# A decoder layer on one core: the q and k stacks built through DRAM from doubled, contiguous stores

## The reference

```
q = (query @ Wq.T + bq).reshape(B, T, H, D)      # H = 16, D = 16
k = (key   @ Wk.T + bk).reshape(B, S, H, D)
scores = einsum('bhtd,bhsd->bhts', q, k) * scale + attn_mask + 2 * bias_of_head
probs  = softmax(scores);  out = einsum('bhts,bhsd->bhtd', probs, v) @ Wo.T + bo
x = x + attn(ln(x));  x = x + xattn(ln(x), ctx);  x = x + ffn(ln(x))
```

## Time and profile before

| | us |
|---|---|
| three runs: median (lowest, highest) | 2261.62 (2259.73, 2263.55) |
| profiled execution, its own time | 2262.71 |
| span of its trace | 2260.9 |
| TensorE matmuls busy | 2077.8 |
| ScalarE busy | 2024.0 |
| VectorE busy | 1860.7 |
| GpSimd busy | 1780.8 |

### The profile page before, as it was taken

One profiled execution on the slowest core, in us unless ns is written; L12 is line 12 of the kernel. 1 busy time (PEld: TensorE's weight loads), 2 busy tenths in 40 slices (PEclk: granted clock), 3 DMA queues, 4 the chain that ended last, 5 costly groups with the idle time before them and its releaser, 6 DMA issues.

```text
span 2260.9 us, 73067 instructions
## 1 busy us (share of the span) xinstructions
PE 2077.8 (92%) x24128; PEld 1806.0 (80%) x24128; DVE 1860.7 (82%) x6768; ACT 2024.0 (90%) x5937; POOL 1780.8 (79%) x1899
## 2 busy tenths in 40 slices
PE   4679999999999999999999999999999999999877
PEld 2568888888888888888888888888888888888755
DVE  4578888888888888888888888888888888888763
ACT  5689999999999999999999999999999999999862
POOL 2358888888888887888888888888888888777863
PEclk9789999999999999999999999999999999999987
DMA  4388778778877779767776887677788777789860
GB/s 142 114 191 175 159 156 172 162 170 188 172 157 154 175 157 175 183 162 169 163 173 156 182 185 164 165 169 169 161 176 187 159 168 165 169 152 183 172 129 15
DMA packets 711784, 367.16 MB, mean 162 GB/s; under 512 B 561392, under 2 KB 659952, under 8 KB 711408
## 3 DMA queue, kind: packets, MB, share of 16 engines
q1 hardware_dynamic: 711408, 362.50, 72.4%
HBM read 202.98 MB, written 25.17 MB: 101 GB/s over the span
## 4 chain that ended last, share of the span: by engine, by line
PE 61%; issue 11%; POOL 10%; ACT 8%; DMA 5%; DVE 5%; SPq 1%; ACTq 0%; DVEq 0%; POOLq 0%
PE ps_c_hidden L978 15%; PE ps_a_misc L978 14%; PE ps_c_out L978 14%; PE ps_b_misc L1115 5%; DMA b_probsT_hi_lo<-b_probs_hi_lo 5%; PE ps_b_scores L1101 3%; POOL bias L522 3%; PE ps_a_misc L1057 3%; ACT c_relu L684 2%; PE ps_a_scores L1038 2%; ACT ps_b_probs L658 2%; POOL ctxT_hi L488 2%; ACT a_qT_hi L603 1%; POOL a_qT_lo L480 1%; POOL ctxT_lo L491 1%
## 5 line engine op out<-in xcount | busy, mean ns | idle before, releaser
L522 POOL TENSOR_TENSOR bias<-bias,b_mask 128x512 f32<-128x512 f32 x512 | 645.0, 1274 | 6.2 <-DMA bias<-in_bias 5.8
L838 DVE CUSTOM_DVE_ANT_0 b_neg_scores<-ps_b_scores,bias 128x256 f32<-128x256 f32 x1024 | 391.2, 419 | 68.3 <-POOL bias L522 34.2
L845 DVE TENSOR_TENSOR b_probs_hi_lo<-ps_b_probs,b_probs_hi_lo 128x512 f16<-128x512 f32 x512 | 351.7, 687 | 107.3 <-ACT b_probs_hi_lo L666 104.9
L543 POOL TENSOR_TENSOR c_hidden_lo<-c_hidden,c_hidden_hi 128x512 f16<-128x512 f32 x288 | 335.1, 1163 | 48.4 <-issue 32.8
L978 PE MATMUL ps_c_hidden<-c_xT_hi,w_hi 128*128 128x256 f16 x1152 | 317.2, 275 | 19.9 <-ACT c_relu L684 19.9
L536 POOL TENSOR_TENSOR c_hidden<-c_relu 128x512 f32<-128x512 f32 x288 | 299.7, 1041 | 32.4 <-ACT c_relu L684 13.1
L978 PE MATMUL ps_c_out<-w_hi,c_hidden_hi 128*128 128x256 f16 x1152 | 315.6, 274 | 9.9 <-DVE acc L949 9.9
L978 PE MATMUL ps_c_hidden<-c_xT_hi,w_lo 128*128 128x256 f16 x1152 | 316.8, 275 | 0.0
L978 PE MATMUL ps_c_hidden<-c_xT_lo,w_hi 128*128 128x256 f16 x1152 | 316.7, 275 | 0.0
L978 PE MATMUL ps_c_out<-w_hi,c_hidden_lo 128*128 128x256 f16 x1152 | 315.9, 274 | 0.0
L978 PE MATMUL ps_c_out<-w_lo,c_hidden_hi 128*128 128x256 f16 x1152 | 315.8, 274 | 0.0
(11 more groups left out here) (194 smaller groups left out, 7491.0 us busy)
## 6 DMA issues: line engine op xcount, KB each, us to landing
bias<-in_bias SPq DMA_DIRECT2D x256, 512.0 KB, 4.2
q_stack<-qk_scratch SPq DMA_DIRECT2D x256, 64.0 KB, 2.5
x_ln<-in_x SPq DMA_DIRECT2D x32, 256.0 KB, 4.4
ctxT<-in_ctx SPq DMA_DIRECT2D x32, 256.0 KB, 4.4
x<-in_x SPq DMA_DIRECT2D x32, 256.0 KB, 5.5
qk_scratch<-b_qT_hi_lo SPq DMA_DIRECT2D x32, 256.0 KB, 4.5
qk_scratch<-b_kT_hi_lo SPq DMA_DIRECT2D x32, 256.0 KB, 3.7
k_stack_even<-qk_scratch SPq DMA_DIRECT2D x128, 64.0 KB, 2.5
```

What stands on the lines that cost most here:

```text
L522: gp.tensor_tensor(part, part, b_mask[:, :], ALU.add).then_inc(b_c_ok, 1)
L543: gp.tensor_tensor(c_hl[:, u, :], c_h[:, :], c_hh[:, u, :], ALU.subtract).then_inc(c_h_ok, 1)
L838: last = dve.tensor_tensor_reduce(out=b_t[:, u, c, :], in0=ps_bs[:, c * T:(c + 1) * T], in1=bias[:, slot, at:at + T], scale=-2.0, scalar=3 ...
L845: dve.tensor_tensor(b_p2[:, j % DEPTH, :, 1, :], ps_bp[:, :].rearrange("p (c t) -> p c t", c=CT), b_p2[:, j % DEPTH, :, 0, :], ALU.subtrac ...
```

## The change

Two things change together. On the host, the columns of Wq and Wk (and their biases) are permuted, so that the projection puts the 16 features of all even heads into partitions 0 to 63 and those of all odd heads into 64 to 127, with the pairs next to each other. And the scratch tensor in DRAM gets the layout of the stacks themselves: half (even or odd head), row of the stack, feature, pair, tokens. Each store writes one half of the partitions to two of the four rows of the stack, so every part is written twice, in pieces of 1 KB: four stores for q and four for k, where there was one each. Each stack is then read by DMAs whose source is contiguous: one for `q_stack` (128 partitions x 4 KB) and one for each k stack (64 partitions x 4 KB), where there were sixteen. The semaphore counts follow.

```diff
             def b_store_k(b, _):
                 sp.wait_ge(b_kl_ok, after(b, 1, 1))
                 carry_waits(sp)
-                sp.wait_ge(b_kst_ok, after(b, STACK, 0))
-                sp.dma_start(stk_d[1].rearrange("r m p t -> p r m t"), b_k2[:, :, :, :]).then_inc(b_k_dram, 16)
+                sp.wait_ge(b_kst_ok, after(b, 32, 0))
+                for h in range(2):
+                    for u in range(2):
+                        sp.dma_start(stk_d[1, h].rearrange("(r u) d g m t -> u (d g) r (m t)", u=2)[u],
+                                     b_k2[64 * h:64 * h + 64, :, :, :].rearrange("p r m t -> p r (m t)")).then_inc(b_k_dram, 16)

             def b_store_q(b, _):
                 sp.wait_ge(b_ql_ok, after(b, 1, 1))
                 carry_waits(sp)
-                sp.wait_ge(b_qst_ok, after(b, STACK, 0))
-                sp.dma_start(stk_d[0].rearrange("r m p t -> p r m t"), b_q2[:, :, :, :]).then_inc(b_q_dram, 16)
+                sp.wait_ge(b_qst_ok, after(b, 16, 0))
+                for h in range(2):
+                    for u in range(2):
+                        sp.dma_start(stk_d[0, h].rearrange("(u r) d g m t -> u (d g) r (m t)", u=2)[u],
+                                     b_q2[64 * h:64 * h + 64, :, :, :].rearrange("p r m t -> p r (m t)")).then_inc(b_q_dram, 16)

             def b_stack_k(b, _):
-                sp.wait_ge(b_k_dram, after(b, 16, 16))
+                sp.wait_ge(b_k_dram, after(b, 64, 64))
                 carry_waits(sp)
                 sp.wait_ge(b_s_ps, after(b, BH, 0))
-                for head, k in enumerate((k_even, k_odd)):
-                    for r in range(4):
-                        at = 64 * head + BD * r
-                        sp.dma_start(k[at:at + BD, :, :],
-                                     stacked(1, r % 2, head)).then_inc(b_kst_ok, 16)
+                for h, k in enumerate((k_even, k_odd)):
+                    sp.dma_start(k[64 * h:64 * h + 64, :, :],
+                                 stk_d[1, h].rearrange("r d g m t -> (r d) (g m) t")).then_inc(b_kst_ok, 16)

             def b_stack_q(b, _):
-                sp.wait_ge(b_q_dram, after(b, 16, 16))
+                sp.wait_ge(b_q_dram, after(b, 64, 64))
                 carry_waits(sp)
                 sp.wait_ge(b_s_ps, after(b, BH, 0))
-                for head in range(2):
-                    for r in range(4):
-                        at = 64 * head + BD * r
-                        sp.dma_start(q_stack[at:at + BD, :, :],
-                                     stacked(0, r // 2, head)).then_inc(b_qst_ok, 16)
+                sp.dma_start(q_stack[:, :, :],
+                             stk_d[0].rearrange("h r d g m t -> (h r d) (g m) t")).then_inc(b_qst_ok, 16)
...
+    rows_of = np.array([[(2 * (2 * g + m) + h) * BD + d for h in range(2) for d in range(BD) for g in range(PAIRS // CD)]
+                        for m in range(CD)]).reshape(D)
     wpair = [chunks(a["L0_attn_Wq"].T), chunks(a["L0_attn_Wk"].T), chunks(a["L0_attn_Wv"].T),
-             chunks(a["L0_xattn_Wq"].T), chunks(a["L0_xattn_Wk"].T), chunks(a["L0_xattn_Wv"].T),
+             chunks(a["L0_xattn_Wq"].T[:, rows_of]), chunks(a["L0_xattn_Wk"].T[:, rows_of]), chunks(a["L0_xattn_Wv"].T),
...
-        "bq": a["L0_xattn_bq"].reshape(CD, P).T,
-        "bk": a["L0_xattn_bk"].reshape(CD, P).T,
+        "bq": a["L0_xattn_bq"].reshape(D)[rows_of].reshape(CD, P).T,
+        "bk": a["L0_xattn_bk"].reshape(D)[rows_of].reshape(CD, P).T,
...
-    args.append(nc.dram_tensor("qk_scratch", (2, 2, CD, P, T), F16, kind="Internal").ap())
+    args.append(nc.dram_tensor("qk_scratch", (2, 2, 4, BD, P // (2 * BD), CD, T), F16, kind="Internal").ap())
```

More of the change, by code:

```diff
@@ L298, in build @@
         FIX = 7
-        STACK = 16 * 8
         def carry_waits(eng):
@@ L388, in b_store_q @@
                 carry_waits(sp)
-                sp.wait_ge(b_qst_ok, after(b, STACK, 0))
-                sp.dma_start(stk_d[0].rearrange("r m p t -> p r m t"), b_q2[:, :, :, :]).then_inc(b_q_dram, 16)
-            def stacked(kind, part, head):
-                return stk_d[kind, part].rearrange("m (p h d) t -> h d (m p) t", h=2, d=BD)[head]
+                sp.wait_ge(b_qst_ok, after(b, 16, 0))
[3 more added lines that the diff above has]
+                                     b_q2[64 * h:64 * h + 64, :, :, :].rearrange("p r m t -> p r (m t)")).then_inc(b_q_dram, 16)
             def b_stack_k(b, _):
-                sp.wait_ge(b_k_dram, after(b, 16, 16))
+                sp.wait_ge(b_k_dram, after(b, 64, 64))
                 carry_waits(sp)
                 sp.wait_ge(b_s_ps, after(b, BH, 0))
-                for head, k in enumerate((k_even, k_odd)):
-                    for r in range(4):
-                        at = 64 * head + BD * r
-                        sp.dma_start(k[at:at + BD, :, :],
-                                     stacked(1, r % 2, head)).then_inc(b_kst_ok, 16)
+                for h, k in enumerate((k_even, k_odd)):
+                    sp.dma_start(k[64 * h:64 * h + 64, :, :],
+                                 stk_d[1, h].rearrange("r d g m t -> (r d) (g m) t")).then_inc(b_kst_ok, 16)
             def b_stack_q(b, _):
-                sp.wait_ge(b_q_dram, after(b, 16, 16))
+                sp.wait_ge(b_q_dram, after(b, 64, 64))
                 carry_waits(sp)
                 sp.wait_ge(b_s_ps, after(b, BH, 0))
-                for head in range(2):
-                    for r in range(4):
-                        at = 64 * head + BD * r
-                        sp.dma_start(q_stack[at:at + BD, :, :],
-                                     stacked(0, r // 2, head)).then_inc(b_qst_ok, 16)
+                sp.dma_start(q_stack[:, :, :],
+                             stk_d[0].rearrange("h r d g m t -> (h r d) (g m) t")).then_inc(b_qst_ok, 16)
             def b_pT_load(b, j):
@@ L496, in b_split_k @@
                 gp.wait_ge(b_kf_ok, after(b, 2, 2))
-                gp.wait_ge(b_k_dram, after(b, 16, 0))
+                gp.wait_ge(b_k_dram, after(b, 64, 0))
                 gp.tensor_tensor(b_k2[:, 1, :, :], b_kf[:, :, :], b_k2[:, 0, :, :], ALU.subtract).then_inc(b_kl_ok, 1)
@@ L503, in b_split_q @@
                 gp.wait_ge(b_qf_ok, after(b, 2, 2))
-                gp.wait_ge(b_q_dram, after(b, 16, 0))
+                gp.wait_ge(b_q_dram, after(b, 64, 0))
                 gp.tensor_tensor(b_q2[:, 1, :, :], b_qf[:, :, :], b_q2[:, 0, :, :], ALU.subtract).then_inc(b_ql_ok, 1)
@@ L632, in b_kv @@
                 act.wait_ge(b_k_ps, after(b, 1, 1))
-                act.wait_ge(b_k_dram, after(b, 16, 0))
+                act.wait_ge(b_k_dram, after(b, 64, 0))
                 for m in range(CD):
@@ L639, in b_q @@
                 act.wait_ge(b_q_ps, after(b, 1, 1))
-                act.wait_ge(b_q_dram, after(b, 16, 0))
+                act.wait_ge(b_q_dram, after(b, 64, 0))
                 for m in range(CD):
@@ L1095, in b_s @@
                 if j == 0:
-                    pe.wait_ge(b_qst_ok, after(b, STACK, STACK))
-                    pe.wait_ge(b_kst_ok, after(b, STACK, STACK))
+                    pe.wait_ge(b_qst_ok, after(b, 16, 16))
+                    pe.wait_ge(b_kst_ok, after(b, 32, 32))
                 pe.wait_ge(b_t_ok, after(b, BH, j))
```

## The result

The changed kernel takes 2288.28 us (median of four runs: 2282.74, 2282.86, 2293.69, 2293.97) against 2261.77 of the kernel before, measured beside it: ratio 1.0118, interval 1.0082 to 1.0153. It is slower by 1.2%. The prediction was 2284 us, within 2258 to 2306. The profiled execution is the one of 2293.97 us, with a span of 2292.2; the four runs lie in two pairs 11 us apart.

The account below looks back on a forecast made before the run. TensorE's wait for head 15's transposition, queued behind the q store, was taken to bound each batch; 14.5 and 7.7 us of added waits made 22.2, so 2262.7 became 2284.9, as a median 2284 us, range 2258 to 2306.

Parts of the forecast that it names:

- What is added at this wait is added to the batch, one to one: TensorE's wait for head 15's transposition, behind the q store: a 2.0 us wait makes a 65.59 us period into 67.67.
- 0.85 us later per landing: Head 15's transposition behind the q stores: 256 KB more in the DMA engines delay its landing by 0.85 us, bounds 0 and 1.44.
- the sum: Added waits for the transposition: 14.5 us in 17 batches already waiting, 7.7 in 14 others, together 22.2 us.
- From one issue to the next the queue takes 0.48 us: SyncE's queue at the q stores: four issues for one put the transposition's issue 1.44 us later, 1.92 after the first store.
- the issue counts in full: Rival: with the backlog drained, the transposition lands 1.44 us later, 40 us in all, 2302 us; chance 0.12.
- mostly hidden: The transposition's later issue is mostly covered by the DMA backlog ahead of it, so the data decides its landing.
- Half stores at half rate: Rival: 64-partition stores move at half rate, halfway 1.9 us later per landing, 55 us in all, 2316 us; chance 0.12.
- Nothing changes: Rival: time goes by pieces and the issue is hidden; landing within 0.1 us, 2263 us; chance 0.16.
- Faster: Rival: larger, later k store and reads stop disturbing the transposition; half of 22.7 us of waits goes, 2250 us; chance 0.10.
- 2 us or more: Last k read of the stack should land at least this long before TensorE's first score product of the batch.
- A faster stack gains nothing there: Stack reads before the first score product: already in time by under a microsecond, so landing 2 us earlier gains nothing.

Follow-up runs that it names:

- e1: Changed kernel with head 15's transposition issued ahead of the four q stores; 2243.99 us, ratio 0.9916.
- e6: Kernel before, with its q store issued twice at full width, the second copy to scratch that nothing reads; 2302.12 us, ratio 1.0181.
- e7: Changed kernel with q and k stored by two 128-partition DMAs each, same 512 KB, scratch laid out by row, then partition; 2397.88 us, ratio 1.0604.
- e9: e7 with each 64-partition stack read cut into four reads of 16 partitions; 2298.17 us, ratio 1.0152.
- e5: Kernel before, with its q store cut into four half-width DMAs, same 256 KB, nothing doubled; 2268.49 us, ratio 1.0029.
- e10: Changed kernel without the doubling: two half-width stores each for q and k, 256 KB in 1-KB pieces, twelve reads; 2256.86 us, ratio 0.9976.
- e2: Kernel before, with head 15's transposition issued ahead of the one q store; 2260.88 us, ratio 0.9988.

## Why the prediction came out right, step by step

**The place and the sign.** "What is added at this wait is added to the batch, one to one" held to within 0.4 us in 24 of the changed kernel's 30 periods; in five of the others a fall of the clock came on top. TensorE now waits for the transposition in all 31 batches behind a q store, as forecast, and for 41.3 us against a forecast of about 45. That the order of this one transfer is the whole of it is shown by e1: with it first, the k store, the reads, the permuted columns and the counts cost nothing.

**The size of the term.** 0.85 us later per landing was forecast, 0.70 is the mean measured (6.30 to 7.00). By bytes alone it is 0.96 (e6). Whether the pieces of 1 KB give some of that back is not shown: e7 and e9 store the 512 KB of e6 in such pieces and full width and land at 7.04 and 7.16 against 7.26, but within each of these kernels the landings scatter by more than half a microsecond. The landings did not all move by the same amount, as the sum had it: they spread from 5.19 to 8.21 before and from 6.28 to 7.72 after, the early ones moving most. The steady part of the account is 18.7 us of waits where the sum had 22.2.

**What was missed.** The falls of TensorE's clock, 7.9 us of the profiled execution, are in no step of the prediction, nor are the 2 us spread over the other periods and the 2.6 before and after them. In the profiled execution the waits came out 3.5 us below the sum and these 12.6 on top, 31.3 where 22.2 were forecast. The median of the runs is 26.5 above the kernel before, since two of the four are 11 us shorter. That 2284 comes as near to 2288.28 as it does is in part luck: the faster pair alone would have made it too high by 1, the slower one too low by 10. The kernel before has waits of up to 2.2 us without a fall between its second and last store, and no row of it told that longer stalls would bring any.

**The issues.** "From one issue to the next the queue takes 0.48 us" was taken from a full-width store and is wrong for a half-width one: 0.63 and the gap. The transposition is issued 3.16 us after the first store, 1.2 later than forecast. By the forecast's own reckoning, 3.16 + 3.5 = 6.7, the issue alone would bring the landing close to the 7.0 that was measured, so the argument that the backlog hides it had hardly any margin left. The rival that the issue counts in full is refuted by e5 (0.28 us on average for 2.2), but "mostly hidden" was too strong: the same run shows that four issues alone cost 5.1 us of waits. It did no further harm here because the doubled bytes alone bring the landing to the same place (e7, e9).

**The other rivals.** *Half stores at half rate* is refuted: full-width stores of the same bytes land the transposition at 7.04 (e7) and 7.16 (e9), half-width ones at 7.00. The Trainium skill (SBUF — State Buffer, "Door 1: The DMA port swizzle") would have them limited to half of the ports; for these stores, at the 247 GB/s of the whole mix, the trace does not show it. That a narrower limit exists when nothing else moves was not tried. *Nothing changes* went by the count of pieces, 512 before and after; that the landing moved by 0.70 all the same refutes it, in e7 (0.74) as well. *Faster* fell: the fewer reads behind the transposition did not bring its landing forward. e10, with 256 KB and fewer, larger pieces, lands only 0.17 us earlier than the kernel before, which its scatter does not resolve.

**The stack.** In the batch shown the last k read lands at 1106.2 + 4.3 = 1110.5, and the first score product loads at 1111.73: 1.2 us of slack. That is the least of the 30 batches; on average the slack is 3.0 us where the kernel before has 1.2 (0.1 at least). So "2 us or more" held on average and not everywhere. But the faster stack is only a part of it. The last k read lands 14.6 us after the first q store where it took 15.5, 0.9 earlier and not 2, because the landing takes 4.3 us for 256 KB where 64 KB took 2.4; the other 0.9 us is TensorE's own lateness, which comes from the wait. "A faster stack gains nothing there" is true for the order as it was and false beyond it. In the kernel before, the stack was the next thing to be late, by about a microsecond, and e2 shows it: take the first wait away and the second takes most of it back. That step should have been put as "gains nothing as long as the transposition is late".

## What to carry to other kernels

A transfer that nobody waits for still has a price if it stands ahead, in the same queue, of one that is waited for: count the bytes ahead of the critical landing, and move that landing first. Then ask what is late next, since two edits that are each worth nothing or less, here three or twelve reads for sixteen and one swapped entry, can together be worth 0.9%. And look at the leading dimension of a DMA on both sides: reads with 4 in front, where 16 was to be had, cost this kernel 100 us.

## What the runs showed of the hardware

- **Few engines.** DMAs whose source leads with a dimension of 4 kept 0.22 to 0.27 of the sixteen DMA engines busy, at about 90 GB/s; with 16 in front the waits behind them fell from 83.7 us to 1.7 (e7, e9). The Trainium skill (DMA: Bandwidth & Descriptors, "Why a DMA increments its semaphore by 16 and not by 1") says that a DMA goes to the largest number of engines, up to 16, that divides the slowest dimension of both its sides. By that it is 4 of 16, 0.25, and the shares of 0.27 and 0.22 agree; which engines carried the packets the traces don't tell.
- **The issue's price depends on the shape.** A store of 64 partitions holds SyncE's queue for 0.63 us, one of 128 partitions with twice the bytes for 0.38. The issue of a transposition takes 1.25 us in the median, and up to 3.7 in the kernel before and 4.2 in e1.
- **The clock after a wait.** Behind waits of 1.78 to 2.29 us TensorE's granted clock fell to half, 1.2 GHz, for 3.4 us in five batches of the changed kernel (0.53 over the window shown); between the second and the last q store none of its waits up to 1.55 us brought a fall. But the kernel before has waits of up to 2.2 us without one. In e9 the falls come behind waits of 1.71 to 2.53 us while others of up to 2.10 pass without, and in e6 behind waits of 1.64 to 2.22 while 2.35 and 2.79 pass. What tells them apart was not found.
